# Expert slots as 128 + 64 rows, a one-hot table with the tiles innermost, and a scatter wait moved to the next scatter

## The reference, cut to what matters

```python
choice = sigmoid(x @ Wg.T) + e_bias                 # 128 experts
topk_idx = top_k(choice, 6)                         # six experts for a token
w = normalised sigmoids of those six * 2.5
# each expert takes its first CAP = 192 tokens, in the order of the tokens
xb = x[token_buf].reshape(E, CAP, 192)
g, u = split(xb @ W_gate_up, 2)                     # 464 hidden features each
yb = (silu(g) * u) @ W_down * w_buf                 # back to 192 features
routed = zeros.at[token_buf].add(yb)
out = h + routed + silu(x @ Wsg) * (x @ Wsu) @ Wsd  # h: the residual rows
```

## Time and profile before

| | us |
|---|---|
| median of 3 runs | 946.81 (944.99 to 950.73) |
| profiled execution, time / span | 954.78 / 953.0 |
| stages of the tokens, ranks and first tables | 0 to 738 |
| expert loop, 20 visits | 738 to 943.5 |
| busy over the span: TensorE / VectorE / ScalarE / GpSimd | 89% / 79% / 36% / 32% |
| mean granted TensorE clock | 0.965 of full |

### The profile page before, as it was taken

How to read it: one execution, slowest core, us unless ns; L and a number is a source line. 1 busy time by engine, 2 the same in 40 slices (tenths; PEclk the granted TensorE clock), 3 DMA queues, 4 the chain that set the end, 5 groups by cost and what they waited for, 6 DMA issues and landing times.

```text
span 953.0 us, 22207 instructions
## 1 busy us (share of the span) xinstructions
PE 846.6 (89%) x7603; PEld 766.5 (80%) x7603; DVE 750.6 (79%) x3738; ACT 343.4 (36%) x971; POOL 308.2 (32%) x350
## 2 busy tenths in 40 slices
PE   1787899899899899899899999998999999999993
PEld 1676688788798788788799999988878878878782
DVE  4256899999899899899999896988635666676662
ACT  0325554553553554544544435331100222122220
POOL 6021212412412312312313311031102556656564
PEclk8799999999999999999999999999986999999997
DMA  7410010110001001001101000001104455565541
GB/s 204 127 51 1 2 35 16 37 32 21 29 20 33 29 17 35 30 17 35 29 19 35 26 20 27 25 25 41 45 5 112 115 143 147 128 152 142 128 115 29
DMA packets 48663, 54.25 MB, mean 57 GB/s; under 512 B 8981, under 2 KB 41595, under 8 KB 48540
## 3 DMA queue, kind: packets, MB, share of 16 engines
q1 hardware_dynamic: 39372, 44.23, 16.3%
q0 software_dynamic: 6592, 7.28, 4.8%
q10 hardware_dynamic: 2608, 1.60, 0.7%
HBM read 42.40 MB, written 10.69 MB: 56 GB/s over the span
## 4 chain that ended last, share of the span: by engine, by line
DVE 41%; PE 28%; issue 11%; POOL 7%; DMA 7%; ACT 3%; SPq 2%; DVEq 0%; POOLq 0%; ACTq 0%
DVE b_arena L1497 10%; POOL b_arena L1758 4%; DMA out_rows<-b_hid,b_add_index 3%; POOL out_rows L1788 3%; DMA out_rows<-b_inner,b_add_index 3%; DVE b_top_a L1483 3%; PE p_big L685 3%; PE p_big L686 2%; DVE b_top_d L1483 2%; PE p_shared L830 2%; DVE b_top_c L1483 2%; PE p_shared L831 2%; DVE b_top_b L1483 2%; DVE b_rstd L1235 2%; PE p_small L866 2%
## 5 line engine op out<-in xcount | busy, mean ns | idle before, releaser
L1758 POOL DMA_INDIRECT b_arena<-x_rows,b_index x44 | 75.0, 1705 | 103.4 <-issue 66.3
L1541 DVE TENSOR_TENSOR b_arena<-b_iota_b,b_slot 128x1152 bf16<-128x1152 bf16 (+1 forms) x46 | 85.2, 1855 | 15.0 <-issue 15.0
L685 PE MATMUL p_big<-b_xT,b_ff1a 128*128 128x128 f32 x384 | 77.7, 285 | 1.4 <-ACT b_xT L1025 1.4
L686 PE MATMUL p_big<-b_xT,b_ff1b 128*128 128x128 f32 x384 | 76.9, 283 | 0.0
L1692 POOL TENSOR_TENSOR b_arena<-b_kY,b_mask_k 64x256 f32<-64x256 f32 x16 | 9.8, 611 | 204.8 <-ACT b_kY L1050 204.8
L1025 ACT COPY b_xT<-p_small 128x256 f32<-128x256 f32 (+1 forms) x97 | 35.5, 377 | 83.2 <-PE p_small L676 83.1
L1723 POOL TENSOR_TENSOR b_arena<-b_arena 128x768 f32<-128x768 f32 x16 | 27.0, 1690 | 117.6 <-DVE b_arena L1509 117.6
L685 PEld LDWEIGHTS p_big<-b_xT,b_ff1a 128*128 128x128 f32 x384 | 61.8, 200 | 2.5 <-ACT b_xT L1025 2.5
L686 PEld LDWEIGHTS p_big<-b_xT,b_ff1b 128*128 128x128 f32 x384 | 61.1, 200 | 0.0
L996 PE MATMUL p_big<-b_xeT,b_arena 128*116 128x192 f32 x320 | 60.1, 331 | 0.0
L719 PE MATMUL p_big<-b_arena,b_q_blk 128*128 128x256 f32 (+3 forms) x256 | 48.9, 334 | 12.4 <-ACT b_q_blk L1057 12.4
(11 more groups left out here) (367 smaller groups left out, 2589.6 us busy)
## 6 DMA issues: line engine op xcount, KB each, us to landing
b_arena<-in_w_gate_up SPq DMA_DIRECT2D x20, 464.0 KB
b_arena<-in_w_down SPq DMA_DIRECT2D x20, 336.0 KB
b_xp<-in_xp SPq DMA_DIRECT2D x16, 384.0 KB, 3.1
b_arena<-in_w_gate_up SPq DMA_DIRECT2D x40, 116.0 KB
xT_rows<-b_xmT SPq DMA_DIRECT2D x16, 128.0 KB, 1.8
b_xT_late<-xT_rows SPq DMA_DIRECT2D x16, 128.0 KB, 2.2
h_rows<-b_h SPq DMA_DIRECT2D x16, 96.0 KB, 1.6
x_rows<-b_xm SPq DMA_DIRECT2D x32, 48.0 KB, 2.0
```

The costliest lines, as they stand in the source:

```text
L685: mm(o, ff1a[:, c * 128:(c + 1) * 128], xTa[s][:], start=True, stop=False)
L686: last = mm(o, ff1b[:, c * 128:(c + 1) * 128], xTb[s][:], start=False, stop=True)
L1541: last = tt(hot[s][:, tiles, :], iota_b[:, None, :].to_broadcast([128, n, CAP]), slot[:, tiles, bass.ds(e, 1)].to_broadcast([128, n, CAP]) ...
L1758: G.indirect_dma_start(xg[s][:, h, :], None, x_rows[:, :], bass.IndirectOffsetOnAxis(index[s][:, h:h + 1], 0)).then_inc(S(f"gathered{s}"), 16)
```

## The change

Slots are split as 128 + 64 instead of 96 + 96: gathers, transposes, indices and scatters take 128 and 64 rows. The table gets the tiles as its innermost axis, 18 of them (17 and a pad, NTP), and 256 slots, of which the last 64 are zeros, cleared once by GpSimd; its two pieces are the slots 0 to 95 and 96 to 191, for all tiles, and both are made after the gate steps of half 1. `slot` is kept as [p, e, t], and the number table `iota_t` is as large as the hot table. The slot products take 128 stationary columns with a step of 18 elements. The down products are made for 128 slots as before, and for the last 64 with the chunks c even and odd in the lower and the upper half of the output partitions; ScalarE scales and copies the 128 rows and the even sum (`y_early`), VectorE adds the odd sum and gives `y_done`. GpSimd waits for `added` of the previous visit ahead of its scatters, gives `add_done` there, and starts with a count of 1 instead of 2. The zero rows are stored from GpSimd's queue instead of SyncE's.

```diff
@@ -30,10 +30,12 @@
 NSC, NIC = IS // SC, I // SC
 DX = D + DB
 HS = CAP // 2
+PARTS = (slice(0, 128), slice(128, CAP))
+HOT = 256
 NT = TILES + 1
+NTP = NT + 1
 DUMMY = T
 ROWS = T + CAP
-HOT_FIRST = 6
 AHEAD = 4
 LATE = 9
 LIST = E + 4
@@ -399,9 +401,9 @@
         cls_before_f = arena[1][0:B, 512:512 + TILES * 128]
         pat_before_f = arena[1][:, 0:TILES * B]
         iota_f = sb("iota_f", [128, CAP + 1])
-        iota_b = sb("iota_b", [128, CAP], bf16)
+        iota_t = sb("iota_t", [128, CAP, NTP], bf16)
         tok_f = sb("tok_f", [128, NT * 3])
-        dummy_f = sb("dummy_f", [HS, 2])
+        dummy_f = sb("dummy_f", [128, 2])
         eval_f = sb("eval_f", [128, 2])
         before = sb("before", [128, 128], bf16)
         cls_before = sb("cls_before", [B, TILES * 128], bf16)
...
@@ -501,21 +503,21 @@
         n_pairs = sb("n_pairs", [1, 1])
 
 
-        hot, at = carve(0, 128, NT, CAP, dt=bf16)
+        hot, at = carve(0, 128, HOT, NTP, dt=bf16)
         rhs = two("rhs", [128, NT, 6], bf16)
-        slot_a, slot_b = two("slot_a", [HS, 2]), two("slot_b", [HS, 2])
-        slot_w, add_w = two("slot_w", [HS, 2]), two("add_w", [HS, 2])
-        index, add_index = two("index", [HS, 2], i32), two("add_index", [HS, 2], i32)
+        slot_a, slot_b = two("slot_a", [128, 2]), two("slot_b", [128, 2])
+        slot_w, add_w = two("slot_w", [128, 2]), two("add_w", [128, 2])
+        index, add_index = two("index", [128, 2], i32), two("add_index", [128, 2], i32)
         xeT = two("xeT", [128, 2, CAP])
         w_gu, at = carve(at, DA, 2 * I)
         w_gu_late, at = carve(at, 2 * DB, I)
         w_dn, at = carve(at, SC, NIC, D)
-        xg, at = carve(at, HS, 2, DX)
+        xg, at = carve(at, 128, 2, DX)
         einner, at = carve(at, SC, NIC, CAP)
         assert at <= 5760
 
         eth = [hid0[0:SC, 0:2 * CAP], inner_buf[0:SC, 0:2 * CAP]]
-        y = [x[0:HS, 384:384 + 2 * D].rearrange("p (h d) -> p h d", d=D) for x in (hid0, inner_buf)]
+        y = [x[:, 384:384 + 2 * D].rearrange("p (h d) -> p h d", d=D) for x in (hid0, inner_buf)]
 
         big = [pb(f"big{s}", [128, 2, 512]) for s in range(2)]
         small = [pb(f"small{s}", [128, 512]) for s in range(3)]
@@ -607,8 +609,6 @@
                     sp.wait_ge(presets, 1)
                 for dst, src in group:
                     sp.dma_start(dst, src).then_inc(done, 16)
-            sp.dma_start(x_rows[T:ROWS, :].rearrange("(p r) d -> p (r d)", r=2), zrows[:]).then_inc(S("zero_rows"), 16)
-            sp.dma_start(out[T:ROWS, :].rearrange("(p r) d -> p (r d)", r=2), zrows[:, 0:2 * D]).then_inc(S("zero_rows"), 16)
 
             sp.sem_inc(S("x_stored"), 64)
@@ -924,7 +924,7 @@
                 pe.wait_ge(S("hot_ready"), v)
                 for h in range(2):
                     for t in range(NT):
-                        last = mm(lists_bank[s][0:HS, 400 + 6 * h:406 + 6 * h], hot[s][:, t, h * HS:(h + 1) * HS], rhs[s][:, t, :],
+                        last = mm(lists_bank[s][:, 400 + 6 * h:406 + 6 * h], hot[s][:, 128 * h:128 * h + 128, t], rhs[s][:, t, :],
                                   start=(t == 0), stop=(t == NT - 1))
                 last.then_inc(S("index_mm"), 1)
@@ -932,8 +932,9 @@
                 pe.wait_ge(S(f"gathered{s}"), gather_value)
                 for h in range(2):
                     for k in range(2):
-                        last = tr(lists_bank[s][:, k * CAP + h * HS:k * CAP + (h + 1) * HS],
-                                  xg[s][:, h, k * 128:(k + 1) * 128], ident[0:HS, 0:HS])
+                        rows = PARTS[h].stop - PARTS[h].start
+                        last = tr(lists_bank[s][:, k * CAP + 128 * h:k * CAP + 128 * h + rows],
+                                  xg[s][0:rows, h, k * 128:(k + 1) * 128], ident[0:rows, 0:rows])
                 last.then_inc(S("xe_T"), 1)
 
             def ranks():
@@ -971,6 +972,7 @@
                 mm(o[:, 2 * LIST:2 * LIST + LIST // 2], ones[:, 0:1], pick[:, 0:LIST:2], start=True, stop=True)\
                     .then_inc(S("list_mm"), 1)
                 yield "pick0"
+                pe.wait_ge(S("hot_cleared"), 1)
                 slots_of(0, 1)
                 yield "pick1"
                 slots_of(1, 2)
@@ -1007,11 +1009,12 @@
                     pe.wait_ge(S("y_done"), v)
                     for r in range(2):
                         pe.wait_ge(S(f"einner{r}"), v + 1)
-                        for h in range(2):
-                            for c in range(2 * r, 2 * r + 2):
-                                last = mm(aux[s][0:HS, h * D:(h + 1) * D],
-                                          einner[s][:, c, h * HS:(h + 1) * HS], w_dn[s][:, c, :],
-                                          start=(c == 0 and h == 0), stop=(c == NIC - 1 and h == 1))
+                        for c in range(2 * r, 2 * r + 2):
+                            mm(aux[s][:, 0:D], einner[s][:, c, 0:128], w_dn[s][:, c, :], start=(c == 0), stop=False)
+                        for c in range(2 * r, 2 * r + 2):
+                            half = slice(64 * (c % 2), 64 * (c % 2) + 64)
+                            last = mm(aux[s][half, D:2 * D], einner[s][:, c, 128:CAP], w_dn[s][:, c, :],
+                                      start=False, stop=(c >= NIC - 2))
                     last.then_inc(S("down_mm"), 1)
@@ -1192,9 +1195,8 @@
                     rows_in(1 - s, v + 1)
                     act.wait_ge(S("kept"), v)
                     act.wait_ge(S("down_mm"), v + 2)
-                    for h in range(2):
-                        last = f(y[s][:, h, :], aux[s][0:HS, h * D:(h + 1) * D], ACT.Copy, scale=add_w[s][:, h:h + 1])
-                    last.then_inc(S("y_done"), 1)
+                    f(y[s][:, 0, :], aux[s][:, 0:D], ACT.Copy, scale=add_w[s][:, 0:1])
+                    f(y[s][0:64, 1, :], aux[s][0:64, D:2 * D], ACT.Copy, scale=add_w[s][0:64, 1:2]).then_inc(S("y_early"), 1)
 
 
         @block.vector
@@ -1407,7 +1409,7 @@
                 yield
                 V.tensor_copy(pat_before[:], pat_before_f)
                 V.tensor_copy(eval_b[:], eval_f[:])
-                V.tensor_copy(iota_b[:], iota_f[:, 1:CAP + 1])
+                V.tensor_copy(iota_t[:], iota_f[:, 1:CAP + 1].unsqueeze(2).to_broadcast([128, CAP, NTP]))
                 yield
                 for s in range(2):
                     V.tensor_copy(rhs[s][:, :, 0:3], tok_f[:].rearrange("p (t c) -> p t c", c=3))
@@ -1536,18 +1538,17 @@
 
                 e = dve.value_load(lists[0:1, bass.ds(j, 1)] if not isinstance(j, int) else lists[0:1, j:j + 1],
                                    min_val=0, max_val=E)
-                for tiles in (slice(0, HOT_FIRST), slice(HOT_FIRST, NT)):
-                    n = tiles.stop - tiles.start
-                    last = tt(hot[s][:, tiles, :], iota_b[:, None, :].to_broadcast([128, n, CAP]),
-                              slot[:, tiles, bass.ds(e, 1)].to_broadcast([128, n, CAP]), ALU.is_equal)
-                    if tiles.stop == NT:
+                for n in range(2):
+                    part = slice(n * HS, (n + 1) * HS)
+                    tt(hot[s][:, part, :], iota_t[:, part, :], slot[:, bass.ds(e, 1), :].to_broadcast([128, HS, NTP]), ALU.is_equal)
+                    if n:
                         V.tensor_copy(rhs[s][:, :, 3:6], wsplit[:, :, bass.ds(e, 1), :].squeeze(2)).then_inc(S("hot_ready"), 1)
                     yield
 
             def indices_of(s, v):
 
                 dve.wait_ge(S("index_mm"), v)
-                p = lists_bank[s][0:HS, 400:412].rearrange("p (h c) -> p h c", c=6)
+                p = lists_bank[s][:, 400:412].rearrange("p (h c) -> p h c", c=6)
                 stt(slot_a[s][:].unsqueeze(2), p[:, :, 2:3], 1.0, dummy_f[:].unsqueeze(2), ALU.subtract, ALU.mult)
                 V.reduce_sum(slot_w[s][:].unsqueeze(2), p[:, :, 3:6], axis=AX.X)
                 V.tensor_copy(slot_b[s][:].unsqueeze(2), p[:, :, 1:2]).then_inc(S("index_part"), 1)
@@ -1567,7 +1568,7 @@
                 yield "slots_out"
                 for b in range(TILES // 4):
                     dve.wait_ge(S("slots_mm"), b + 1)
-                    stt(slot[:, 4 * b:4 * b + 4, 0:E], big[b // 2][:, b % 2, :].rearrange("p (t e) -> p t e", e=E), 1.0,
+                    stt(slot[:, 0:E, 4 * b:4 * b + 4].rearrange("p e t -> p t e"), big[b // 2][:, b % 2, :].rearrange("p (t e) -> p t e", e=E), 1.0,
                         chosen[:, 4 * b:4 * b + 4, :], ALU.add, ALU.mult).then_inc(S("slots_done"), 1)
                     yield
                 yield "rank"
@@ -1637,9 +1638,10 @@
                             ts(add_w[s][:], slot_w[s][:], 0.5, None, op0=ALU.mult).then_inc(S("kept"), 1)
                             dve.wait_ge(S("kept"), v)
                             indices_of(s, v + 2)
-                        if r == 0:
-                            next(slots)
                     run(slots)
+                    dve.wait_ge(S("y_early"), v)
```

(29 more changed lines are left out.)

10 lines of the change are left out of this document (5 added, 5 removed).

## The result

The changed kernel takes 958.66 us (median of 4, 957.53 to 960.68), the kernel before beside it 946.29 (944.99 to 950.73): a ratio of 1.0125, 95% interval 1.0086 to 1.0163. It is slower: the interval lies above 1, though the difference is only a little over 1%. The time is 30 us above the forecast of 928.5. The profiled execution took 959.36 (span 957.5).

A forecast was written before the change was run, and what follows sets the result against it. VectorE's table and GpSimd's descriptors, holding each other up, were taken to bound the loop. A visit falling from 9.96 to 9.1 us gives -16.3, one-time parts +0.5 - 1.5 - 1: -18.3 off the 946.81 median, 928.5 us; range 915 to 949.

The forecast's parts named there:

- The slot products: TensorE's 34 products per visit with the one-hot table: from 1.55 to 1.3 us, bounds 1.0 to 2.1.
- the step of 36 bytes slows the weight reads: Rival for TensorE's slot products: 3.8 us a visit, period 11.6, 977 us in all; chance 0.10.
- The transposes: TensorE's transposes, 128 + 64 rows instead of 96 + 96: no change, with 0.2 us either way.
- The down products: TensorE's second expert products: from 3.00 to 2.5 us a visit, bounds 2.2 to 3.4.
- the pair: Two 64-column down products on different halves of the output partitions run together: 0.33 us instead of 0.7.
- The longer path through the gate steps: Second up products, tanh, gate steps, second half of down products: would set the visit at 9.1 us, above TensorE's 8.7.
- The start of the sum: The loop's visit before the change, 9.96 us from the profiled execution; falling to 9.1 gives 16.3 us over 19 visits.
- One-time parts: Outside the repeating visits: iota cast +0.5 us, earlier first table -1.5, last scatters no longer held up -1.
- the early visit: Visit from 747.39 to 756.87 in the profile before: TensorE never waits, so its own sum is 9.48 us.
- the ring: VectorE's table and GpSimd's gathers, scatters and indices hold each other up, setting the 9.97 us period before the change.
- the cover of VectorE's added step: VectorE's sum of the pair's halves, 0.4 us, is done 0.7 us before the next visit's tanh, so hidden.
- removing the landing wait alone: GpSimd's wait for the scatter to land, some 1.7 us beyond issue, lies in time blocked anyway: no gain.

The follow-up runs named there:

- e15: The change as it is, run again on one chip with the kernel before: 959.05 us, ratio 1.0125.
- e13: The kernel before, unchanged, profiled once more: 945.53 us in its one execution.
- e3: The change with the table laid out and its pieces placed as before, loading 128 adjacent columns: 942.75 us, 0.9844 of the kernel before at 960.03.
- e14: The kernel before with only GpSimd's scatter wait moved and zero rows on its queue, repeated on another chip: 944.25 us, ratio 0.9972.
- e1: The kernel before with only GpSimd's scatter wait moved and zero rows on its queue: 945.60 us, 0.9875 of the kernel before at 960.03.
- e11: The kernel before with tile pairs innermost, table pieces after the gate steps and 128-column loads, wait and zero rows unmoved: 935.99 us, ratio 0.9898.
- e16: The kernel before with moved wait, tile pairs innermost, table pieces after the gate steps, loads kept at 96 columns: 937.75 us, ratio 0.9914.

## Why the prediction was wrong

The forecast was a gain of 18.3 us, worked out on the profiled execution of 954.78 and taken off the median; e15 lies 13.6 above e13 by span (957.3 against 943.7). The 31.9 between divide so:

- **The slot products** were the step that failed: priced at 38 ns and 1.3 us, with bounds of 1.0 to 2.1, while the text itself said that no row shows the step. They took 2.13, +0.83 a visit. The rival "the step of 36 bytes slows the weight reads" named the mechanism and overrated its price (3.8 us). It drew it from before's slowest 34 products, which ran at half clock (granted 0.50 from 720 to 728 us); this said nothing of a step. The argument that a load of 128 columns took 96 ns where one of 96 took 125 was right for adjacent columns (0.87 us in e3) and did not carry over. That the upper bound of 2.1 nearly holds is luck: it stood for a price by the column, and e3, with as many columns, takes 0.87. By the same luck the period of 10.05 lies inside the bounds of 8.6 to 10.1; that the time lies above the range of 915 to 949 all the same comes from the start of the sum and the clock, below.
- **The transposes** at nothing +- 0.2: +0.25. **The down products** at 2.5: 2.65, since a full-width one takes 0.42, not the 0.375 of the 96-column ones; the pair was right (0.5 a half expected, 0.47 measured). **The first up products** behind the 64-row pairs: +0.09. With the slots +1.32 on TensorE's own sum of 8.73, which gives the 10.05. The longer path through the gate steps (9.1) never closed: no wait of 0.3 to 0.4 us appeared. By its own terms, with the measured slot and down products put in, it comes to about 10.0 (estimate), just under TensorE's 10.05. Against the 9.1 forecast the period is 0.95 too long, 18.1 us in 19 visits.
- **The start of the sum**: 9.96 a visit, from an execution known to lie 8 above the median, while the result was taken off the median. A usual execution runs at 9.54 (e13), so 19 x 0.42 = 8.0 us of the gain did not exist. The profiled surplus had to be looked for in the loop before it was subtracted.
- **The clock**: 4.6 us in the three longer visits of e15 and 1.6 in its last one, 6.2 in all, not foreseen.
- **One-time parts**: -2 expected. The first up products of the loop start 1.9 us earlier than in e13, as foreseen for the first table. From the last slot products to the end it is 1.2 longer, of which the clock is 1.6, so 0.4 shorter without it: -2.3 in all, -0.3 against the forecast.

Together 18.1 + 8.0 + 6.2 - 0.3 = 32.0.

The slot products alone turned the gain into a loss. With 1.3 us for them and everything else as measured, TensorE's sum would be 9.22 us against the 9.54 of before: 19 x 0.32 = 6 us less, with the one-time parts some 938 us (an estimate, without falls of the clock). The start of the sum was the second error. Two readings of before were off as well, at no cost to the sum: the early visit holds a wait (above), and the terms of the ring add up to 10.05, not 9.97, because the next second piece starts at 845.39, 0.08 ahead of the gate product's end.

Right were the table (1.06 a piece), the gathers, the cover of VectorE's added step (0.42, no wait for it on TensorE), and that GpSimd would leave the chain. That removing the landing wait alone "buys nothing while the ring stands" nearly holds on usual executions: e14 gains 0.07 us a visit, 0.3% in all. It was not so for the slower rhythm, from which the prediction argued: a visit of 9.96 becomes one of 9.47 in e1, which gained 1.25% on the chip on which the kernel before ran at 960. What the sentence missed besides is e11: once the table is short, the wait is worth some 14 us.

By the Trainium skill (TensorE: Matmul & The Clock Gate, "Weight-path perf modes"), a load of 128 columns of a type other than fp32 is fast, also with a step. The runs agree in part: 128 columns beat 96 at either layout (25.6 against 46 ns adjacent, 62.6 against 180 at 36 bytes), but the step takes back more than the fast load gives. By the Trainium skill (SBUF — State Buffer, "Door 1: The DMA port swizzle"), two accesses in each 16-byte line are needed for full speed. At 4 bytes (25.6 ns) and at 18 (60.6) the runs agree; at 8 bytes, where two columns still share a line, they do not (34.1).

## What to carry to other kernels

A layout has two readers. Before the writer's side is priced, look for a row in which the other side reads with that step; if there is none, the bound has to reach to several times the adjacent price, or the layout is to be cut so that the step stays small (here pairs of tiles: the whole table gain, no price on the loads). Where two resources bound a loop almost equally, parts of a change are worth little alone and much together: the moved wait alone 0.3%, with wide loads still 0.3%, with a short table instead 0.9% (e16), with both 2.5%. And when a profiled execution lies above the median, find the surplus in it before taking differences.
